# Another order of steps for the turn and the opening of the first attention

## The chip, the cores and the metric

The kernel runs on one core of one Trainium2 chip. The metric is the device time of one execution in microseconds (us), as the median over several runs. The engines are PE (TensorE), DVE (VectorE), ACT (ScalarE) and POOL (GpSimd); SP (SyncE) issues most of the DMAs. Each engine executes its own instruction stream in order and waits on semaphores.

## The reference

The program is a causal attention over 8 sequences of 512 tokens with 256 channels and 16 heads of 16, followed by a sum with the input and a layernorm, and then two layers of windowed attention and feed-forward. Only the first attention is touched:

```python
qkv = x @ w_qkv + b_qkv                      # x: 8 x 512 x 256
q, k, v = split_heads(jnp.split(qkv, 3))     # 16 heads of 16
a = (q @ k.T + causal_mask) / sqrt(16)
z = softmax(a) @ v
x = layernorm(x + (z @ w_out + b_out))
```

## The kernel before

The first attention handles one sequence (b = 0 to 7) at a time. Its work on a sequence is cut into named steps, and a step holds instructions for several engines. Steps that begin with `f_` belong to the "front" of the next sequence, the others to the sequence in hand. A loop of 7 turns executes the list `STEPS`; in it the front steps work for sequence b+1 while the rest finishes sequence b. Before the loop the list `OPENING` makes the front of sequence 0, and after it a list of joins finishes sequence 7 beside the first steps of the next stage. `follow` gives the same list to every engine: an engine takes the steps in the list's order and leaves out those in which it has nothing to do. So the list sets the order on each engine by hand, and nothing is reordered at run time.

The steps, with the engine's work in each:

- `f_x`: SP loads the sequence into `xin`; PE turns it (L576). `f_xe`: ACT writes `a_xt_hi` (L410), DVE `a_xt_lo` (L474).
- `f_qk:0` to `f_qk:3`: PE projects a quarter of q and k (L554 to L556), six matmuls each. `f_qe:i`: ACT makes `a_qk_hi` and `a_part_f` from it (L422, L426), POOL subtracts `a_qk_lo` (L371), and SP stores the three parts to the scratch tensor `qk_parts` (L304, L306).
- `f_load:i`: SP loads a quarter of the stacked `a_Q` and `a_K` from `qk_parts` (L322, four DMAs). Loads 0 and 1 need the stores of `f_qe:0` and `f_qe:1`, loads 2 and 3 those of `f_qe:2` and `f_qe:3`; in the loop, load i also waits until PE has finished the last `st` that reads the old quarter (`st:5`, `st:11`, `st:17`, `st:23`).
- `sm:i` and `f_sm:i` (32 of them): PE makes the scores of two heads for 128 queries (L631, mask L637) in one of two banks, DVE takes the negated maxima (L491). PE's `sm:i` waits for the maxima of `sm:i-2`. `f_sm:0`, `f_sm:8`, `f_sm:16` and `f_sm:24` wait for loads 0, 1, 2 and 3.
- `mt:i` and `f_mt:i`: PE turns the maxima (L663), ACT copies them to `a_mrow` (L445), SP puts them into `a_Q` (L327).
- `st:i` and `f_st:i` (24 of them): PE makes the scores again, turned (L676, L681), ACT takes the exponential into `a_PT` (L454). `ms:i` and `f_ms:i`: POOL masks blocks on the diagonal (L379).
- `pv:i` (4): PE multiplies by the values (L704). `z0:i` to `z3:i`: DVE turns and divides the result (L510, L512, L516), POOL (for the last one DVE) splits it (L384, L386), DVE turns it back (L529), ACT rounds it (L435).
- `f_v:i`: PE projects the values, DVE adds the bias (L497).
- `xr`: POOL loads the residual input, and DVE adds the output bias to it (L502). `out:i`: PE projects the output (L720, L722), DVE adds the residual (L536) and takes statistics. `end`: ACT normalises, POOL stores the rows.
- `nw` (opening only): SP loads the next stage's weights and stores rows of zeros.

PE, DVE and ACT share four single banks of PSUM; two of them (`FB`) serve the projections, `mt`, `pv` and `out` in turn, so that for example `f_qk:2` waits until ACT has read `f_qk:0` out.

Of the kernel before, what the change touches and what calls it, by code (L numbers as in the profile page):

```python
# [114 lines left out]
def parse(text):  # L115
    return [(name, int(i)) for name, i in (s.rsplit(":", 1) for s in text.split())]
# [67 lines left out]
def first_attention(nc, ctx, K, at, banks, scr, w, xin, rows_out, zeros, ahead, x, w_qkv, b_qkv, w_out, b_out, dst):  # L184
# [37 lines left out]
    xr = put(188480, "xr", [P, TB, DM])  # L222
    y, out = put(192576, "y", [P, TB, DM]), rows_out
    st, mv = sb("st", [P, TB, 6]), sb("mv", [P, TB, 2])
# [37 lines left out]
    GM, GE = PG * TB, PG * 3  # L262

    STEPS = parse("""
        f_xe:0 f_x:0 sm:27 st:8 sm:28 xr:0 mt:2 st:9 f_qe:0 f_qk:0 f_qk:1 f_qe:1 st:10 sm:29 ms:2 f_qk:2 ms:3
        f_load:0 sm:30 f_load:1 st:11 sm:31 f_qe:2 pv:0 st:12 z0:0 mt:3 f_qe:3 z1:0 f_qk:3 st:13 pv:1 f_sm:0
        st:14 f_sm:1 f_sm:2 st:15 f_sm:3 st:16 f_sm:4 st:17 f_sm:5 f_sm:6 st:18 f_sm:7 st:19 ms:4 f_sm:8 st:20
        z2:0 f_sm:9 f_sm:10 st:21 f_sm:11 ms:5 z0:1 ms:6 f_sm:12 st:22 z1:1 f_mt:0 f_sm:13 z3:0 st:23 z2:1
        pv:2 z0:2 f_sm:14 ms:7 z1:2 f_st:0 f_ms:0 f_load:2 f_load:3 f_sm:15 z0:3 pv:3 z3:1 z2:2 f_st:1 f_v:0
        z1:3 f_st:2 z3:2 f_mt:1 f_sm:16 z2:3 f_sm:17 f_st:3 f_v:1 f_sm:18 f_v:2 z3:3 f_sm:19 out:0 out:1  # L270
        f_sm:20 f_st:4 out:2 out:3 f_st:5 f_ms:1 f_sm:21 f_sm:22 f_st:6 f_sm:23 f_st:7 end:0 f_sm:24 f_v:3
        f_sm:25 f_sm:26""")
    FIRST = [s for s in STEPS if s[0][0] == "f"]
    OPENING = parse("""
        f_x:0 f_qk:0 nw:0 f_xe:0 f_qk:1 f_qk:2 f_qe:0 f_qk:3 f_qe:1 f_load:0 f_sm:0 f_sm:1 f_sm:2 f_sm:3
        f_qe:2 f_sm:4 f_sm:5 f_sm:6 f_qe:3 f_sm:7 f_load:1 f_load:3 f_sm:8 f_sm:9 f_sm:10 f_mt:0 f_ms:0
        f_sm:11 f_sm:12 f_v:0 f_sm:13 f_sm:14 f_st:0 f_sm:15 f_load:2 f_st:1 f_sm:16 f_sm:17 f_st:2 f_sm:18
        f_sm:19 f_mt:1 f_sm:20 f_st:3 f_sm:21 f_v:1 f_st:4 f_v:2 f_st:5 f_sm:22 f_sm:23 f_v:3 f_ms:1 f_st:6
        f_sm:24 f_sm:25 f_st:7 f_sm:26""")

    def sync(sp):
        sp.dma_start(xin[:, :, :], x[0].rearrange("(t p) d -> p t d", p=P)).then_inc(x_in, 16)
# [1463 lines left out]
def program(nc, t, out):  # L1746
# [7 lines left out]
    with ExitStack() as ctx:  # L1754
# [8 lines left out]
             for i in range(DEPTH)]  # L1763
# [4 lines left out]
                                   t["L0_ffn_ln_b"][i], t["L0_ffn_w1"][i], t["L0_ffn_b1"][i], t["L0_ffn_w2"][i],  # L1768
                                   t["L0_ffn_b2"][i]) for i in range(DEPTH)]
        stage, left = first_attention(nc, ctx, K, at, banks, scr, w[0], xin, rows_out, zeros, local[0], t["L0_attn_x"],  # L1770
                                      t["L0_attn_w_qkv"], t["L0_attn_b_qkv"], t["L0_attn_w_out"], t["L0_attn_b_out"],
                                      after_first)
# [44 lines left out]
```

## Time and profile before

| | us |
|---|---|
| median of 3 runs | 1787.78 (1783.2 to 1791.49) |
| the profiled execution | 1787.27 |
| its span in the profile | 1785.7 |
| PE busy | 1704.7 (95%) |
| DVE busy | 1150.5 (64%) |
| ACT busy | 997.9 (56%) |
| POOL busy | 866.6 (49%) |
| mean granted TensorE clock | 0.963 of full |

The opening takes the first 56 us, the seven turns of the loop run until about 446 us, and the rest belongs to the joins and the four stages behind. A turn is counted here from the first matmul of `f_x` to the next such matmul. "Full" clock is 2.4 GHz, and a granted clock of 0.50 is 1.2 GHz.

### The profile page before, as it was taken

What the parts mean: (1) busy time and instruction counts of PE and PEld (TensorE: products, weight loads), DVE (VectorE), ACT (ScalarE), POOL (GpSimd) and SP (SyncE); (2) the same over time, 40 slices, a digit from 0 to 9 for tenths busy, and PEclk for the clock granted to TensorE, in tenths of its full rate; (3) what the DMA queues carried; (4) which work ended last, traced back from release to release, by engine and by line L of the source; (5) the groups of instructions that cost most, each with busy time, mean ns of one, the idle gap of its engine ahead of it and who ended that gap; (6) DMA issues with size and microseconds to landing.
All of it is one profiled execution on the core that took longest, in us unless ns stands there. A gap on an engine that the chain in (4) does not pass through costs nothing.

```text
span 1785.7 us, 42024 instructions
## 1 busy us (share of the span) xinstructions
PE 1704.7 (95%) x13984; PEld 1305.2 (73%) x13984; DVE 1150.5 (64%) x2853; ACT 997.9 (56%) x1927; POOL 866.6 (49%) x886
## 2 busy tenths in 40 slices
PE   5999999999799999999989999899999999999997
PEld 3667566666477777777768888677777777778886
DVE  6678777787876676766643443876766776545554
ACT  2556576566545565555554555565555655655443
POOL 3343344434644665644643333556445656445453
PEclk7898898989989999999999999999999999999999
DMA  7454554544211011110023122101110010222221
GB/s 224 132 134 121 147 165 142 144 124 122 61 48 37 0 35 35 35 35 23 2 83 118 62 67 72 60 14 35 35 35 6 29 35 23 84 70 84 94 82 48
DMA packets 102327, 129.64 MB, mean 73 GB/s; under 512 B 15834, under 2 KB 70788, under 8 KB 102276
## 3 DMA queue, kind: packets, MB, share of 16 engines
q1 hardware_dynamic: 96084, 106.44, 20.5%
q0 software_dynamic: 6192, 22.55, 3.6%
q8 instruction: 29, 0.48, 0.1%
q14 instruction: 22, 0.18, 0.0%
HBM read 82.55 MB, written 46.15 MB: 72 GB/s over the span
## 4 chain that ended last, share of the span: by engine, by line
PE 81%; DVE 6%; DMA 4%; issue 3%; ACT 3%; POOL 1%; SPq 1%; DVEq 0%; POOLq 0%; ACTq 0%
PE b L1210 8%; PE d L1104 6%; PE b L1235 6%; PE d L1105 5%; PE d L1106 5%; PE d L631 3%; PE d L1151 3%; PE b L676 3%; PE d L1176 3%; PE b L704 3%; PE d L1623 2%; PE d L1625 2%; PE d L1624 2%; PE b L1250 2%; DMA a_K<-qk_parts 2%
## 5 line engine op out<-in xcount | busy, mean ns | idle before, releaser
L454 ACT ACTIVATE a_PT<-b 128x384 f32<-128x384 f32 (+1 forms) x384 | 183.6, 523 | 151.3 <-PE b L676 99.5
L491 DVE TENSOR_REDUCE a_negm<-d 128x2 f32<-128x256 f32 (+3 forms) x256 | 201.1, 814 | 67.1 <-PE d L637 65.3
L907 POOL TENSOR_TENSOR l_t<-l_t,l_t 128x512 f32<-128x512 f32 x128 | 165.0, 1297 | 113.4 <-DVE l_t L1059 113.3
L1077 DVE CUSTOM_DVE_ANT_0 d<-d,window 128x256 f32<-128x256 f32 (+1 forms) x512 | 184.4, 422 | 24.9 <-PE d L1176 24.6
L1476 POOL TENSOR_TENSOR m_hid_lo<-m_hid,m_hid_hi 128x512 fp32r<-128x512 f32 x80 | 103.3, 1301 | 161.6 <-ACT m_hid_hi L1537 161.5
L991 ACT ACTIVATE l_PT<-b 128x512 f32<-128x512 f32 (+1 forms) x256 | 125.3, 542 | 97.0 <-PE b L1218 95.0
L921 POOL TENSOR_TENSOR l_PS<-l_PT 128x768 f32<-128x768 f32 x64 | 117.6, 1838 | 111.4 <-ACT l_PT L991 111.4
L1104 PE MATMUL d<-w,l_xt 128*128 128x512 f32 x384 | 165.6, 431 | 4.8 <-DVE l_t L1059 4.7
L379 POOL TENSOR_SCALAR_AFFINE_SELECT a_PT<-a_PT 128x512 f32<-128x512 f32 x128 | 80.4, 656 | 180.3 <-ACT a_PT L454 179.6
L1105 PE MATMUL d<-w,l_xt 128*128 128x512 f32 x384 | 152.6, 398 | 0.0
L1106 PE MATMUL d<-w,l_xt 128*128 128x512 f32 x384 | 152.3, 397 | 0.0
L631 PE MATMUL d<-a_K,a_Q 63*128 63x256 f32 (+2 forms) x512 | 123.8, 449 | 24.3 <-DMA a_K<-qk_parts 18.0
L1210 PE MATMUL b<-l_Q,l_K 64*128 64x256 f32 x1536 | 139.2, 293 | 3.3 <-ACT l_PT L991 2.6
L1210 PEld LDWEIGHTS b<-l_Q,l_K 64*128 64x128 f32 x1536 | 108.8, 186 | 42.3 <-ACT l_PT L991 19.6
L914 POOL TENSOR_TENSOR l_qk<-l_t,l_inv 128x512 f32<-128x512 f32 x128 | 131.5, 1050 | 0.0
L1577 DVE SCALAR_TENSOR_TENSOR m_hid<-b,mw_b,m_gate 128x512 f32<-128x512 f32 (+1 forms) x48 | 35.9, 748 | 122.2 <-ACT m_gate L1524 97.3
L954 ACT ACTIVATE l_sq<-d 128x512 f32<-128x512 f32 x128 | 76.7, 599 | 65.5 <-PE d L1106 50.7
L1235 PE MATMUL b<-l_PT,l_V 128*64 128x256 f32 (+1 forms) x1024 | 112.2, 361 | 1.1 <-issue 0.7
L1054 DVE TENSOR_REDUCE l_ss<-l_sq 128x8 f32<-128x512 f32 x128 | 87.2, 681 | 31.2 <-ACT l_sq L954 30.6
L1094 DVE TENSOR_TENSOR rows_out<-b,l_xr 128x256 f32<-128x256 f32 x64 | 27.2, 425 | 123.6 <-PE b L1106 123.6
L1537 ACT ACTIVATE m_hid_hi<-m_hid 128x512 fp32r<-128x512 f32 x96 | 60.6, 631 | 75.1 <-DVE m_hid L1577 75.1
L925 POOL TENSOR_TENSOR l_zl<-l_zt,l_zh 128x512 fp32r<-128x512 f32 x64 | 81.5, 1294 | 39.7 <-ACT l_zh L997 39.7
(222 smaller groups left out, 4885.5 us busy)
## 6 DMA issues: line engine op xcount, KB each, us to landing
qk_parts<-a_qk_hi SPq DMA_DIRECT2D x64, 256.0 KB, 3.4
a_Q<-qk_parts SPq DMA_DIRECT2D x64, 192.0 KB, 3.7
a_K<-qk_parts SPq DMA_DIRECT2D x64, 192.0 KB, 4.6
qk_parts<-a_qk_lo SPq DMA_DIRECT2D x32, 256.0 KB, 4.0
xin<-after_attn SPq DMA_DIRECT2D x32, 256.0 KB, 3.1
m_xr<-after_attn SPq DMA_DIRECT2D x16, 512.0 KB, 3.9
after_attn<-rows_out POOLq DMA_DIRECT2D x14, 512.0 KB, 5.4
xin<-in_L_attn_x SPq DMA_DIRECT2D x8, 512.0 KB, 3.3
```

The source lines that it names most:

```text
L454: nc.scalar.activation(PT[:, p // PG % 2, 2 * (p % PG) + hh, QOFF[t]:QOFF[t] + nq], SC[hh][:, 0:nq], ACT.Exp, scale=AD ** -0.5).then_inc(e ...
L491: dve.tensor_reduce(negm[:, q, 2 * p:2 * p + 2], MX[i % 2][:, :, 0:nk], AX.X, ALU.max, negate=True).then_inc(max_done, 1)
L631: pe.matmul(bank[:, hh, 0:nk], Q[rows, p, P * q:P * q + P], Kk[rows, p, 0:nk], start=True, stop=True)
L907: pool.tensor_tensor(t1[:, par, w, :], t1[:, par, w, :], t2[:, par, w, :], ALU.add)\
L914: pool.tensor_tensor(qk[:, i, w, :].rearrange("p (h d) -> p h d", d=FD), t1[:, par, w, :].rearrange("p (h d) -> p h d", d=FD), inv[:, par, ...
L991: nc.scalar.activation(PT[:, p % 2, hh, j:j + 2, :].rearrange("p j q -> p (j q)")[:, 0:nq], SC[hh][:, 0:nq], ACT.Exp, scale=8.0).then_inc( ...
L1077: m = dve.tensor_tensor_reduce(out=o, in0=o, in1=mask, scale=-1.0, scalar=-NEG, op0=ALU.add, op1=ALU.min, accum_out=negm[:, q + t, p // 2, ...
L1104: pe.matmul(o, a_hi, r_hi, start=first, stop=False)
L1105: pe.matmul(o, a_lo, r_hi, start=False, stop=False)
L1106: return pe.matmul(o, a_hi, r_lo, start=False, stop=last)
L1210: pe.matmul(SC[hh][:, 2 * P * t:2 * P * t + 2 * P], lhs, rhs, start=(t == 0 and n == 0), stop=False, skip_group_check=True)
L1235: pe.matmul(OB[rows, P * j:P * j + nq], V[:, j, FD * h:FD * h + FD], PT[:, i % 2, hh, j, 0:nq], start=(j == 0), stop=(j == TB - 1), skip_g ...
```

## The change

Only the two lists differ. Every step of the old lists is in the new ones, and no instruction is added or removed.

```diff
     STEPS = parse("""
-        f_xe:0 f_x:0 sm:27 st:8 sm:28 xr:0 mt:2 st:9 f_qe:0 f_qk:0 f_qk:1 f_qe:1 st:10 sm:29 ms:2 f_qk:2 ms:3
-        f_load:0 sm:30 f_load:1 st:11 sm:31 f_qe:2 pv:0 st:12 z0:0 mt:3 f_qe:3 z1:0 f_qk:3 st:13 pv:1 f_sm:0
-        st:14 f_sm:1 f_sm:2 st:15 f_sm:3 st:16 f_sm:4 st:17 f_sm:5 f_sm:6 st:18 f_sm:7 st:19 ms:4 f_sm:8 st:20
-        z2:0 f_sm:9 f_sm:10 st:21 f_sm:11 ms:5 z0:1 ms:6 f_sm:12 st:22 z1:1 f_mt:0 f_sm:13 z3:0 st:23 z2:1
-        pv:2 z0:2 f_sm:14 ms:7 z1:2 f_st:0 f_ms:0 f_load:2 f_load:3 f_sm:15 z0:3 pv:3 z3:1 z2:2 f_st:1 f_v:0
-        z1:3 f_st:2 z3:2 f_mt:1 f_sm:16 z2:3 f_sm:17 f_st:3 f_v:1 f_sm:18 f_v:2 z3:3 f_sm:19 out:0 out:1
-        f_sm:20 f_st:4 out:2 out:3 f_st:5 f_ms:1 f_sm:21 f_sm:22 f_st:6 f_sm:23 f_st:7 end:0 f_sm:24 f_v:3
-        f_sm:25 f_sm:26""")
+        f_x:0 f_xe:0 sm:27 xr:0 st:8 mt:2 f_qk:0 f_qk:1 f_qe:0 f_qe:1 f_load:0 f_qk:2 ms:2 st:9 sm:28 f_load:1
+        sm:29 sm:30 st:10 ms:3 sm:31 f_qe:2 pv:0 st:11 mt:3 z0:0 st:12 z1:0 f_qk:3 st:13 f_qe:3 z2:0 pv:1 z0:1
+        st:14 f_sm:0 f_sm:1 st:15 f_load:2 f_sm:2 f_sm:3 st:16 f_sm:4 z1:1 z3:0 st:17 ms:4 f_sm:5 f_sm:6 st:18
+        ms:5 f_sm:7 st:19 f_sm:8 st:20 f_sm:9 ms:6 f_sm:10 f_mt:0 st:21 f_sm:11 f_sm:12 ms:7 st:22 f_load:3
+        f_sm:13 z2:1 f_sm:14 z0:2 st:23 pv:2 z1:2 f_sm:15 f_sm:16 z0:3 pv:3 z3:1 f_st:0 z2:2 f_v:0 f_mt:1 z1:3
+        f_st:1 z3:2 f_sm:17 z2:3 f_v:1 f_st:2 f_sm:18 z3:3 f_v:2 f_st:3 f_sm:19 out:0 f_st:4 f_sm:20 out:1
+        out:2 out:3 f_st:5 f_sm:21 f_ms:0 f_ms:1 f_sm:22 f_st:6 f_sm:23 f_st:7 f_sm:24 f_v:3 end:0 f_sm:25
+        f_sm:26""")
     FIRST = [s for s in STEPS if s[0][0] == "f"]
     OPENING = parse("""
-        f_x:0 f_qk:0 nw:0 f_xe:0 f_qk:1 f_qk:2 f_qe:0 f_qk:3 f_qe:1 f_load:0 f_sm:0 f_sm:1 f_sm:2 f_sm:3
-        f_qe:2 f_sm:4 f_sm:5 f_sm:6 f_qe:3 f_sm:7 f_load:1 f_load:3 f_sm:8 f_sm:9 f_sm:10 f_mt:0 f_ms:0
-        f_sm:11 f_sm:12 f_v:0 f_sm:13 f_sm:14 f_st:0 f_sm:15 f_load:2 f_st:1 f_sm:16 f_sm:17 f_st:2 f_sm:18
-        f_sm:19 f_mt:1 f_sm:20 f_st:3 f_sm:21 f_v:1 f_st:4 f_v:2 f_st:5 f_sm:22 f_sm:23 f_v:3 f_ms:1 f_st:6
-        f_sm:24 f_sm:25 f_st:7 f_sm:26""")
+        f_x:0 f_xe:0 f_qk:0 f_qe:0 f_qk:1 f_qk:2 f_qk:3 f_sm:0 f_sm:1 f_sm:2 f_qe:1 f_load:0 f_sm:3 f_sm:4
+        f_sm:5 f_qe:2 f_load:1 f_qe:3 f_sm:6 f_sm:7 f_ms:0 nw:0 f_sm:8 f_mt:0 f_sm:9 f_sm:10 f_sm:11 f_sm:12
+        f_sm:13 f_st:0 f_sm:14 f_st:1 f_sm:15 f_sm:16 f_load:2 f_st:2 f_sm:17 f_st:3 f_sm:18 f_v:0 f_st:4
+        f_sm:19 f_ms:1 f_load:3 f_mt:1 f_sm:20 f_sm:21 f_sm:22 f_v:1 f_st:5 f_v:2 f_sm:23 f_sm:24 f_st:6 f_v:3
+        f_st:7 f_sm:25 f_sm:26""")
```

## Rows read from the trace of the kernel before

**Rows 1.** The page's granted clock in 40 slices of the span, tenths of full speed

```profile
PEclk7898898989989999999999999999999999999999
```

**Rows 2.** Windows: turns 1, 2 and 4, and the sum of turns 1 to 6

```profile
core 0: us, PE busy (x) PEld busy (x) DVE busy (x) ACT busy (x) POOL busy (x), PEclk, DMA share, GB/s
56.05:114.92 58.87, 55.13 (x491) 36.84 (x489) 40.73 (x69) 34.44 (x70) 19.93 (x30) 0.86 0.47 127
114.92:170.44 55.52, 53.95 (x488) 36.31 (x489) 40.92 (x70) 34.70 (x71) 22.50 (x32) 0.88 0.51 142
...
226.93:279.33 52.40, 50.43 (x488) 33.25 (x489) 40.59 (x70) 34.45 (x71) 22.46 (x32) 1.00 0.52 151
...
sum 335.96, PE 322.58 PEld 213.12 DVE 245.13 ACT 207.78 POOL 132.27; mean PE 53.76 PEld 35.52 DVE 40.85 ACT 34.63 POOL 22.05
```

**Rows 3.** Waits of PE in the loop: us in total, times, longest

```profile
PE d L631 <- DMA a_K<-qk_parts: 9.3, 7, 3.4
PE d L631 <- DVE a_negm L491: 3.4, 15, 0.3
PE b L676 <- DMA a_Q<-a_mrow: 0.5, 1, 0.5
```

**Rows 4.** Timeline of PE: head of turn 2, `f_sm:0` of turn 4 (start, us, instruction, idle)

```profile
114.92 1.09 PE L576 MATMUL b<-ident,xin 128*128 128x128 f32 x8
...
118.21 0.50 PE L554 MATMUL b<-a_xt_hi,w 128*128 128x512 f32 x1
...
121.16 0.45 PE L676 MATMUL b<-a_Q,a_K 64*128 64x384 f32 x2
...
123.33 0.44 PE L631 MATMUL d<-a_K,a_Q 63*128 63x384 f32 x2
...
124.45 0.51 PE L631 MATMUL d<-a_K,a_Q 63*128 63x512 f32 x2 [0.29 <-DVE a_negm L491]
...
130.12 2.36 PE L704 MATMUL b<-a_PT,a_V 128*32 128x512 f32 x32
133.48 0.38 PE L631 MATMUL d<-a_K,a_Q 63*128 63x256 f32 x2 [1.00 <-DMA a_K<-qk_parts]
...
245.24 0.38 PE L631 MATMUL d<-a_K,a_Q 63*128 63x256 f32 x2 [0.76 <-DMA a_K<-qk_parts]
```

**Rows 5.** Timeline of DVE in turn 2, head

```profile
116.24 1.29 DVE L474 TENSOR_TENSOR a_xt_lo<-b,a_xt_hi 128x512 fp32r<-128x512 f32 x2 [0.16 <-ACT a_xt_hi L410]
...
122.35 1.45 DVE L502 TENSOR_TENSOR a_xr<-a_xr,a_bo 128x1024 f32<-128x1024 f32 x1 [3.36 <-DMA a_xr<-in_L_attn_x]
```

**Rows 6.** Timeline of ACT in turn 2: the second copy of `f_qe:0`

```profile
120.58 0.68 ACT L426 ACTIVATE a_part_f<-b,a_bqk 128x512 f32<-128x512 f32 x1
```

**Rows 7.** Timeline of POOL in turn 2: `end`'s store, subtractions of `f_qe:0` and `f_qe:1`

```profile
116.38 0.86 POOL L398 DMA_DIRECT2D after_first<-rows_out  x1 [1.82 <-ACT rows_out L440]
...
121.42 3.50 POOL L371 TENSOR_TENSOR a_qk_lo<-a_part_f,a_qk_hi 128x512 fp32r<-128x512 f32 x2 [3.17 <-ACT a_part_f L426]
```

**Rows 8.** Timeline of SP in turn 2: last store of `f_qe:1`, first of `f_load:0`

```profile
125.09 0.33 SPq L306 DMA_DIRECT2D qk_parts<-a_qk_lo  x1
127.33 0.89 SPq L322 DMA_DIRECT2D a_Q<-qk_parts  x2
```

**Rows 9.** Windows from `f_sm:0` to `pv:2` on PE, turns 2 and 4

```profile
133.48:148.32 14.84, 14.83 (x116) 11.33 (x116) 12.15 (x18) 9.95 (x20) 3.67 (x7) 0.57 0.46 138
...
245.24:257.32 12.08, 11.63 (x116) 8.07 (x117) 10.83 (x16) 9.39 (x20) 3.17 (x6) 1.00 0.53 166
```

**Rows 10.** Timeline of DVE in turn 4, `f_sm:0` to `pv:2`

```profile
245.74 3.62 DVE L491 TENSOR_REDUCE a_negm<-d 128x2 f32<-128x256 f32 x5 [4.88 <-PE d L637]
249.99 3.02 DVE L491 TENSOR_REDUCE a_negm<-d 128x2 f32<-128x512 f32 x4 [0.63 <-PE d L637]
252.92 0.70 DVE L529 STREAM_TRANSPOSE a_ztf<-a_on 128x512 f32<-128x512 f32 x1
...
256.21 0.71 DVE L510 STREAM_TRANSPOSE a_ot<-b 128x512 f32<-128x512 f32 x1
256.95 0.26 DVE L512 RECIPROCAL a_rc<-a_ot 128x16 f32<-128x16 f32 x1
```

**Rows 11.** Timeline of PE in the opening: `f_sm:16`

```profile
43.50 0.58 PE L631 MATMUL d<-a_K,a_Q 63*128 63x256 f32 x2 [0.86 <-DMA a_K<-qk_parts]
```

## The prediction

> **What bounds the kernel now.** I read the page first: PE is busy for 95% of the span, so only what PE waits for, and the clock at which it works, can give time back. The line of the granted clock [rows 1] shows where that is: the slices below 9 lie in the first 400 us, the opening and the loop of the first attention, which are all that the change touches. I therefore cut the loop into its turns [rows 2]. Turn 4 takes 52.40 us at a clock of 1.00; turns 1 and 2 take 58.87 and 55.52 us at 0.86 and 0.88. All have the same work, and PE calls itself busy in the extra time too. The first six turns sum to 335.96 us, and six times 52.40 is 314.4: 21.6 us are lost against the turn without a low clock. By the same view five of the seven turns have a stretch at 0.50, always between `f_sm:0` and the first matmuls of `pv:2`, and turns 4 and 7 have none.
>
> Then I asked what PE waits for in the loop [rows 3]. One wait stands out: 9.3 us in seven waits for the DMA into `a_K`, that is `f_sm:0` waiting for `f_load:0`. One of them, in turn 1, is 3.4 us, the other six average (9.3-3.4)/6 = 0.98. The next is DVE, 3.4 us in 15 small pieces. In turn 2 [rows 4] the wait is 1.00 us ahead of 133.48, right where the dense projections and `pv:1` end and the thin 63-row matmuls begin.
>
> **Step 1: the new head of a turn.** All times here are us from the turn's first matmul, in turn 2 (114.92) [rows 4]. Before, `f_qk:0` starts at 3.29 and `f_sm:0` at 18.56, with waits of 0.29 (`sm:31`) and 1.00 in between. In the new list `sm:28` and `st:9` move behind `f_qk:2`, `st:11` behind `pv:0`, and `st:14` ahead of `f_sm:0`. That is the same work plus `st:14`. Three new waits appear:
>
> - `f_qk:0` needs `a_xt_lo`, whose second half ends at 116.24+1.29, or 2.61 [rows 5]. PE is there at about 2.4 now. A wait of 0.2 to 0.3, and `f_qk:0` starts at about 2.75, 0.55 earlier.
> - `f_qk:2` follows `f_qk:1` directly and needs the second copy of `f_qe:0`, which ended at 121.26 [rows 6], 3.05 behind the start of `f_qk:0`. The two projections between take 121.16-118.21 = 2.95 [rows 4], and a signal needs some 0.1. A wait of 0.1 to 0.2, which `st:10` and `sm:29` covered before.
> - DVE has `xr:0` ahead of `sm:28` now. Its addition waits for a DMA until 7.43 and ends at 8.88 [rows 5]. The maxima of `sm:28` (about 0.4) end at 9.3, and PE needs them for `sm:30`, which it reaches at about 8.5. A wait of 0.8 to 0.9. Queued behind the addition are all later maxima; `sm:31` comes right after with nothing more to wait for.
>
> Together 1.1 to 1.4. I take 1.3; the lower bound is 0.4, if the residual lands at once, and the upper one 2.6, if it lands 1.24 later (rival 3). The step `xr` on POOL comes behind `f_ms:0` and `f_ms:1` now, where one of them stood before; that is 1.24 us more on POOL, hidden in the 1.82 us in which it waited for ACT's normalised rows [rows 7].
>
> **Step 2: the load.** `f_load:0` is ready when the stores of `f_qe:1` have landed. Its chain is `f_qk:0`, ACT, the two subtractions on POOL (3.50 us, stretched while the addition of `xr` runs beside them) [rows 7], the store at 125.09, and 2.24 us until SP issues the load at 127.33 [rows 8], then 6.15 until `f_sm:0` runs. I let the chain move with `f_qk:0`: 0.55 earlier, so the data is there at 18.56-0.55 = 18.0. PE gets there at 18.56-1.00-0.29+1.3+0.45 (`st:14`, by the `st` at 121.16 [rows 4]) = 19.0. The wait is gone, with 1.0 us to spare. SP stays in order: `f_load:1` waits for `st:11` and holds the stores of `f_qe:2` behind it, but SP is occupied by the first load's four issues until then, as before. `f_load:2` and `f_load:3` are issued 9 and 2 steps of scores earlier and are needed at `f_sm:16` and `f_sm:24`; they gain cover.
>
> The head alone is thus no gain: 1.3 of new waits against 0.98+0.29 = 1.27 of old ones. Only turn 1 gains, where of 3.4 about 1.4 stays and some 0.4 of new waits is added (its `xr` is early): -1.6.
>
> **Step 3: between `f_sm:0` and `pv:2`.** In turn 4 this stretch takes 12.08 us and DVE is busy for 10.83 of them [rows 9]; its maxima run in chains of 3.02 us per four, with `z2:0` (0.70) and `z0:1` (0.71 and 0.26) among them [rows 10]. These 1.67 us move ahead of `f_sm:0`, where DVE lay idle for 4.88 us [rows 10]. Against it stand `f_sm:14`, now inside the stretch, and that `z0:1` has to wait for `pv:1` and so delays the first maxima of `f_sm:0` by up to 0.3. For equal work I get 0.3 to 0.5 less than before. The tail behind `pv:3` has the same matmuls against the same DVE work. Its swaps (`f_st`, `f_mt:1`, `out:1`) are covered as long as the additions into `a_V`, `z3:3` and the maxima are done before PE asks; without that cover they cost up to 0.5 a turn. Head, middle and tail together lie between -0.3 and +0.7 a turn; I take the middle, +0.2, or +1.4 for seven turns.
>
> **Step 4: the clock.** This is the main term. The low stretch makes `f_sm:0` to `pv:2` 14.84 us in turn 2 against 12.08 in turn 4 [rows 9]. Of the 21.6 us lost, 2.6 are turn 1's longer wait; the rest, 19.0 in five turns, is 3.8 a turn. In the trace each fall comes in the thin stretch behind the stall, in no turn before it, and a turn with nearly the same stall (0.76 in turn 4 [rows 4]) keeps full speed. So the trace bears out that these turns are close to the edge, and not that the stall alone decides. Two things now make the stretch denser: no DMA wait at its start, and 1.67 us less of DVE's work inside. I expect four of the five falls to go, -15.2, with none (0) and all (-19.0) as bounds. The Trainium skill says in "TensorE: Matmul & The Clock Gate", section "HAM oscillation — how this bites in real kernels", that waits for DMAs between short runs of matmuls are what puts the array back to half rate; by that rule all five would go, and the sum would be 3.8 lower.
>
> **Step 5: the opening.** `f_sm:16` loses its 0.86 us wait for `f_load:2` [rows 11], since more scores stand between `f_mt:0` and it. Moving `nw` back takes its two large loads away from the first stores, but by the time these are issued the loads had landed; nothing. `f_load:1` overtakes the stores of `f_qe:3`, needed only much later. -0.9, within -2 and +1.
>
> **The sum.** The profiled execution took 1787.3 (span 1785.7), half a microsecond from the median of 1787.8. +1.4 (turns 1 to 7), -1.6 (turn 1), -15.2 (clock), -0.9 (opening) is -16.3: 1771. The joins are as they were and begin with the same steps finished.
>
> **The rivals.**
>
> *Rival 1: the low clock stays.* The new waits of step 1 are smaller but three, and the thin stretch itself is the same matmuls. For it: turns 4 and 2 differ by only 0.24 us of stall. Against it: the turn that fell latest (turn 3) fell behind further small waits, one of them of 0.5 for `a_mrow` [rows 3], which now has more cover. Time: 1787.3+1.4-1.6-0.9 = 1786. The skill's page has a section "A second HAM failure mode: psum-queue depth-cycling", by which frequent short idle times between groups of matmuls are enough to make the clock oscillate; it speaks for this rival, and the full-speed turn 4 with its small waits for DVE speaks against its always being so.
>
> *Rival 2: half of it.* Two or three of the five falls go: -9.5 instead of -15.2, 1777.
>
> *Rival 3: slower.* DVE's queue behind the residual. If the residual lands later than 7.43, each microsecond is one more for PE at `sm:30`, in six turns. If POOL's 1.24 us are not hidden, that is +7.4; and if the idle time now in the head lets the clock fall in all seven turns, two more at 3.8 are +7.6. 1786+15 = 1801. It decides once the head loses over 1.7 us a turn beyond step 1 and the clock gives nothing, or half of that with seven falls. For it: the addition already waited 3.36 us [rows 5]. Against it: POOL's wait of 1.82.
>
> **How the numbers follow.** About 0.5%, or 9 us, is what a measurement of this kernel tells from no change. Forecast 0.42, rival 1 0.22, rival 2 0.25, rival 3 0.11. The forecast and four fifths of rival 2 lie more than 9 us below: faster 0.61. Rival 1 and the rest of rival 2 are the same, 0.28; slower 0.11. The range reaches from 1763 (all falls gone, -19.0, and turns 0.3 shorter, -2.1, with the rest as above) to 1790, which holds rivals 1 and 2 with some microseconds for the phase of the clock in other stages. The likeliest case's own range is 1766 to 1777.
>
> **What would show it.** The DMA wait at `f_sm:0` near zero in turns 2 to 7 (step 2); new idle time of PE at `f_qk:2` and at `sm:30`, the latter with DVE's L502 just before (step 1); turns of 52 to 53 us with a clock of 1.00 in at least five of seven, against two before (step 4); `f_sm:0` to `pv:2` below 12.1 us in them (step 3). The prediction is wrong if turns at full clock take over 53.5 us, which would mean that I missed a wait, or if half the turns or more still show 0.50.

## The result: no gain, and a little slower

The changed kernel took 1792.76 us in the median of 12 runs (1779.94 to 1803.25), the kernel before 1786.12 in 12 runs beside it (1778.85 to 1791.93). The ratio is 1.004, with a 95% interval of 1.002 to 1.0059, or some 7 us more (3.6 to 10.5). I had forecast 1771 within 1763 to 1790. The profiled execution of the changed kernel took 1801.12 (span 1799.6) and is itself 8 us above the median; the profile of before lies 1 us above its own.

The page's granted clock in 40 slices, to be held against [rows 1]:

```profile
PEclk7788989988999999999999999999999999999999
```

The windows of turns 1 to 6 of the changed kernel, in the columns of [rows 2]:

```profile
60.92:118.30 57.38, 55.11 (x492) 35.57 (x489) 40.50 (x70) 34.05 (x70) 18.93 (x29) 0.88 0.44 121
118.30:176.48 58.18, 55.77 (x488) 35.07 (x489) 41.06 (x70) 34.65 (x71) 21.41 (x33) 0.88 0.48 136
176.48:230.89 54.41, 51.97 (x488) 33.04 (x489) 41.12 (x70) 34.64 (x71) 21.41 (x33) 0.97 0.52 145
230.89:289.60 58.71, 56.28 (x489) 35.87 (x489) 41.50 (x70) 34.66 (x71) 21.42 (x33) 0.85 0.46 135
289.60:343.95 54.35, 51.93 (x488) 32.85 (x489) 41.24 (x70) 34.64 (x71) 21.40 (x33) 0.97 0.51 145
343.95:401.92 57.97, 55.59 (x489) 35.04 (x489) 41.03 (x70) 34.68 (x71) 21.43 (x33) 0.88 0.46 136
sum 341.00, PE 326.65 PEld 207.44 DVE 246.44 ACT 207.31 POOL 125.99; mean PE 54.44 PEld 34.57 DVE 41.07 ACT 34.55 POOL 21.00
```

The six turns sum to 341.00, against 335.96. No turn has a clock of 1.00 any more; even the two best, 3 and 5, have 0.97 and take 54.4, against 52.40 in turn 4 of before. What PE waits for in the loop, as in [rows 3]:

```profile
PE d L631 <- DVE a_negm L491: 9.7, 8, 1.6
PE b L663 <- DVE a_xt_lo L474: 0.9, 6, 0.2
PE b L676 <- DMA a_Q<-a_mrow: 0.9, 1, 0.9
PE d L631 <- DMA a_K<-qk_parts: 0.3, 1, 0.3
```

The 9.3 us for the DMA into `a_K` are gone, as meant. In their place stand 9.7 us for DVE's maxima, where 3.4 stood. The timeline of turn 3 shows where (this turn begins at 176.48). PE first, from `f_qk:2` on, to be read beside [rows 4]:

```profile
182.23 0.50 PE L554 MATMUL b<-a_xt_hi,w 128*128 128x512 f32 x1
...
186.35 0.44 PE L631 MATMUL d<-a_K,a_Q 63*128 63x384 f32 x2 [1.55 <-DVE a_negm L491]
...
187.45 4.05 PE L704 MATMUL b<-a_PT,a_V 128*32 128x512 f32 x32
```

Then DVE and POOL in the same head, beside [rows 5, 7]:

```profile
183.85 2.11 DVE L502 TENSOR_TENSOR a_xr<-a_xr,a_bo 128x1024 f32<-128x1024 f32 x1 [3.63 <-DMA a_xr<-in_L_attn_x]
185.88 3.11 DVE L491 TENSOR_REDUCE a_negm<-d 128x2 f32<-128x256 f32 x4
```

```profile
182.35 2.53 POOL L371 TENSOR_TENSOR a_qk_lo<-a_part_f,a_qk_hi 128x512 fp32r<-128x512 f32 x2 [2.63 <-ACT a_part_f L426]
```

Two things are to be seen. At `sm:30` PE stands still for 1.55 us until DVE has finished the addition and the maxima of `sm:28`. And `pv:0` right behind it takes 4.05 us, where the same 32 matmuls took 2.36 [rows 4]: the granted clock is 0.50 there. Both are so in turns 2 to 7 (in turn 5 `pv:0` takes 3.87). In turn 1 the residual is there early, the wait is 0.25, and `pv:0` keeps full speed. Besides, the middle of the turn, from `f_sm:0` to `pv:2`, still has its low stretch in five of the seven turns, as before; they are now turns 1, 2, 4, 6 and 7, and were 1, 2, 3, 5 and 6.

The clock's part can be read from every run, not only from the profiled one. It has two levels, 1.00 and 0.50, so a run's low time is twice (1 - mean granted clock) times its span. The mean low time is 121.0 us in 113 runs of the kernel before (standard error 1.2) and 125.2 in 12 of the changed one (4.6).

### The profile page after: what moved, and what is told of

It is laid out like the page before. It is cut to its first block, busy times and chain, and to the rows that moved or that the text cites. A ratio compares the mean times of both kernels' runs of the same rounds, so it can differ in the third digit from the quotient of the medians.

```text
span 1799.6 us, 42024 instructions
## 1 busy us (share of the span) xinstructions
PE 1715.9 (95%) x13984; PEld 1301.8 (72%) x13984; DVE 1153.1 (64%) x2853; ACT 997.9 (55%) x1927; POOL 860.2 (48%) x886
## 4 chain that ended last, share of the span: by engine, by line
PE 80%; DVE 6%; DMA 4%; issue 4%; ACT 3%; POOL 2%; SPq 1%; POOLq 0%; DVEq 0%; ACTq 0%
PE b L1210 8%; PE b L1235 6%; PE d L1104 6%; PE d L1105 5%; PE d L1106 5%; PE b L704 4%; PE d L1151 3%; PE b L676 3%; PE d L631 3%; PE d L1176 2%; PE d L1623 2%; PE d L1625 2%; PE d L1624 2%; PE b L1250 2%; DMA a_xr<-in_L_attn_x 2%
## 5 line engine op out<-in xcount | busy, mean ns | idle before, releaser
L631 PE MATMUL d<-a_K,a_Q 63*128 63x256 f32 (+2 forms) x512 | 115.2, 442 | 22.9 <-DVE a_negm L491 12.8
L1104 PEld LDWEIGHTS d<-w,l_xt 128*128 128x128 f32 x384 | 72.6, 189 | 38.9 <-issue 18.1
```

The lines of the kernel that those rows point to most:

```text
L631: pe.matmul(bank[:, hh, 0:nk], Q[rows, p, P * q:P * q + P], Kk[rows, p, 0:nk], start=True, stop=True)
L1104: pe.matmul(o, a_hi, r_hi, start=first, stop=False)
```

## The experiments

Each kernel's times stand beside runs of the kernel before on the same chip, whose medians lay between 1785 and 1788. A "low time" is a mean over the kernel's runs, with its standard error behind it.

**One part alone.** The first kernel has the old turn and the new opening, the second the new turn and the old opening.

> The old turn with the new opening. Theory 1 (the new opening itself costs: in the profile after, the loop began at 60.92 us and not at 56.05, with the low clock lasting until 62 us and not 51): 4 to 5 us slower than before, about 1791, and the profile again shows the loop beginning near 61. Rival (the later rise of the clock was chance in that one execution): within 2 us of before, and a loop that begins at 55 to 57.

Measured: 1787.24, ratio 1.0017 (0.9996 to 1.0039); low time 126.6 (5.4). PE waits 8.0 us for `a_K`, against 9.3 before, and no head has a low stretch at `pv:0`. The time is that of the rival, but the loop begins at 60.81, as theory 1 said; I come back to this at step 5.

> The new turn with the old opening. Theory 1 (the turn costs about 2 us in sum over seven turns, the opening the rest of 6.6): about 1788, 2 us over before, with the wait of 1.5 us of PE at sm:30 and a stretch at half clock behind it in six turns. Rival (the turn is the whole loss): about 1793.

Measured: 1792.14, ratio 1.0037 (1.0017 to 1.0057); low time 120.0 (4.0). The profile has the waits and the low heads of the changed kernel:

```profile
PE d L631 <- DVE a_negm L491: 10.0, 9, 1.6
```

So the turn alone makes the kernel slower, as the rival said. The opening is within its error of nothing here.

**The addition behind `sm:31`.** The changed kernel with DVE's half of `xr` as a step `xb` of its own, so that `sm:28` to `sm:31` no longer stand behind it on DVE. The same step stands in the joins behind the loop, where the order stays.

```diff
-        sm:29 sm:30 st:10 ms:3 sm:31 f_qe:2 pv:0 st:11 ...
+        sm:29 sm:30 st:10 ms:3 sm:31 xb:0 f_qe:2 pv:0 st:11 ...
```

> The changed kernel, but DVE's addition into a_xr (L502) is a step of its own and comes behind sm:31; POOL still issues its load at the old place. Theory A (the addition ahead of sm:28 makes PE wait 1.5 us at sm:30, and the idle time then lets the clock fall, so that pv:0 takes 4.05 us in place of 2.36): both go, 1.55 + 1.69 = 3.2 us in six turns, 19 us less than the changed kernel, about 1774, and pv:0 takes 2.36 in all turns. Theory B (the clock falls in the head because the thin steps sm:28 to sm:31 now stand together, whatever the wait): only the 1.55 goes, about 1784, and pv:0 stays at about 4.

Measured: 1783.18, ratio 0.9995 (0.9972 to 1.0019), about 8 us below the changed kernel by the ratios; low time 119.4 (6.1). PE's waits for DVE's maxima fall to 2.5 us, none over 0.4. No head is low, and `pv:0` takes 2.36, as theory A said. But 8 us is less than half of its 19. The heads of the profile lose about 20 us of low time (3.4 in each of six), and the mean run only 6, so low time seems to come back elsewhere, within large errors. The addition now runs clear of POOL's subtractions:

```profile
179.95 1.54 DVE L502 TENSOR_TENSOR a_xr<-a_xr,a_bo 128x1024 f32<-128x1024 f32 x1
```

A turn without a low stretch takes 51.5, in the windows of turns 4 and 6 of this kernel:

```profile
223.68:275.16 51.48, 50.32 (x488) 32.64 (x489) 40.84 (x70) 34.65 (x71) 21.56 (x33) 1.00 0.55 153
...
329.46:381.15 51.69, 50.21 (x488) 32.62 (x489) 40.94 (x70) 34.64 (x71) 21.54 (x33) 1.00 0.55 153
```

The head's wait and its low stretch went together, and what came back is about the whole loss of 7 us. But with neither DMA wait nor DVE wait left, the low time is still that of the kernel before. The middle keeps its low stretches, three of seven in this profile.

**The same with the old opening.**

> The turn of e3_addition_late (addition behind sm:31) with the old opening. If what the opening costs (about 3 us) and what the addition costs (about 8 us) add up: 1780, 0.3% faster than before. If the opening's cost was chance: as e3, 1783.

Measured: 1781.3, ratio 0.9985 (0.9961 to 1.0008); low time 119.1 (4.9), and low stretches in the middle of six turns of its profile. The time lies between the two that I had expected and decides for neither.

**A projection between `sm:29` and `sm:30`.** The changed kernel with `f_qk:2` put there.

> The changed kernel with f_qk:2 between sm:29 and sm:30, and the addition where the change put it. Theory A: the projection's 1.4 us fill PE's wait, and the clock stays up in the head; about 1775 to 1778, pv:0 at 2.36. Theory B: the wait is filled as well, and thin steps are now parted by a dense one, so B also says a full clock. Against both: if f_qe:2, now 2 us later, holds back f_load:2, a DMA wait shows at f_sm:16, and the gain is smaller.

Measured: 1798.66, ratio 1.0062 (1.0038 to 1.0085). My expectation was wrong in its reasoning: the work that PE does before `sm:30` is the same in either order, so the wait stayed (10.3 us in all, 1.7 at most). `f_qk:2` only came later. The middle is low in all seven turns of this profile.

**The kernel before, with the addition ahead of `sm:28`.**

```diff
-        ... sm:27 st:8 sm:28 xr:0 mt:2 ...
+        ... sm:27 xr:0 st:8 sm:28 mt:2 ...
```

> The kernel before with one step moved: xr ahead of sm:28, so that DVE's addition stands ahead of the maxima of sm:28 as in the changed kernel. Theory A (that order alone makes PE wait and the clock fall in the head): PE waits for DVE about 1 us at sm:29 or sm:30 in six turns and pv:0 takes over 2.4 us in some; 6 to 15 us slower than before. Rival (the wait only matters because the changed turn puts the projections together ahead of it; here the DMA wait at f_sm:0 shrinks by what PE loses earlier): within 3 us of before.

Measured: 1787.64, ratio 1.0004 (0.9983 to 1.0026); the waits for DVE rise from 3.4 to 6.1, none over 0.8, and no head is low. This is what the rival said: the order on DVE alone, without the projections at the head of the turn, costs nothing that is measured.

**`pv:0` ahead of `sm:30`.** The changed kernel with a block of PE's work that needs nothing of DVE's put in front of the wait.

> The changed kernel with pv:0 ahead of sm:30 in place of behind sm:31; the addition stays ahead. In e4 the projection was moved from one place ahead of sm:30 to another, which gives PE no more to do before it, so its wait stayed at 1.7 us. Here 2.3 us of other work come ahead of sm:30. Theory A: the wait of 1.5 us and the low clock in the head both go, as with e3: about 1784. Theory B (thin steps together): sm:28 to sm:31 are parted as well, so B also says a full clock; if the clock still falls at the same place, both are wrong.

Measured: the 12 runs fall into two groups, six from 1770.5 to 1788.4 and six from 1805.3 to 1808.2 at a clock of 0.951 or 0.952. The ratio of 0.9975 (0.9943 to 1.0008) is over the first six alone; the median over all is 1796.82. Why there are two groups I don't know. In the profile, which is of the first group, the waits for the maxima fall to 0.6 us, another of 0.66 a turn for ACT comes up at `mt:3`, and a turn at full clock takes 52.2. `pv:0` keeps full speed and no middle is low, but in three of seven turns the clock falls behind the new wait of 0.66. The spread makes it no use as a repair.

**Half of the addition.** The changed kernel with the bias added to 512 of the 1024 columns only (the other half goes without).

> The changed kernel with DVE's addition of the output bias to the residual done on half of the columns only (512 of 1024; the other half is left without the bias). The addition takes 2.11 us beside POOL's subtractions and comes down to about 1.1. Theory A (PE's wait at sm:30 is the addition's length on DVE, and the fall of the clock in the head comes with that wait): the wait falls by 1.0 a turn, from 1.6 to about 0.5 (10 us in the loop to about 3.5), the low stretch in the head goes, pv:0 takes 2.36 instead of 4.05, and the kernel is 8 to 10 us faster than the changed one, about 1783. Rival B (it is the late landing of the residual that PE waits for, or the clock falls for another reason): the wait falls by less than 0.5 a turn, the head keeps its low stretch in most turns, and the time stays within 3 us of the changed kernel's.

Measured: 1779.1, ratio 0.9962 (0.9934 to 0.9989); low time 101.8 (6.4). The heads' low stretches are gone and a turn at full clock takes 52.21, as theory A said. But the wait at `sm:30` fell by 0.53, from 1.55 to 1.02, and not by 1.0. DVE and then POOL in turn 3 of this kernel show why:

```profile
178.47 1.67 DVE L502 TENSOR_TENSOR a_xr<-a_xr,a_bo 128x512 f32<-128x512 f32 x1 [3.56 <-DMA a_xr<-in_L_attn_x]
180.06 3.11 DVE L491 TENSOR_REDUCE a_negm<-d 128x2 f32<-128x256 f32 x4
```

```profile
177.05 2.54 POOL L371 TENSOR_TENSOR a_qk_lo<-a_part_f,a_qk_hi 128x512 fp32r<-128x512 f32 x2 [2.65 <-ACT a_part_f L426]
```

The half addition, 0.68 in turn 1 where POOL is elsewhere, takes 1.67 here. It ends 180.14-179.59 = 0.55 behind the end of POOL's second subtraction. The whole one in the changed kernel ends 185.96-184.88 = 1.08 behind it. So the addition is not just slowed down; it stands still until POOL is through, and then needs nearly its own time (1.22 for the whole one in turn 1). All turns say the same. In turns 2 to 7 of the changed kernel it starts between 7.27 and 7.51 behind the turn's first matmul and always ends 1.08 behind POOL's second subtraction. In the kernel before it starts between 6.98 and 7.43 and always ends 1.08 behind the first one. Even the late addition, 1.54 above, ends 181.49-180.42 = 1.07 behind a mask block of POOL's.

**Dense work in the middle.** The turn of the late addition with the old opening, and `f_qk:3` with `f_qe:3` moved behind `st:16`; `f_load:2` and `f_sm:16` go later for it.

> As e6, and the dense projection f_qk:3 (with f_qe:3) moves into the thin stretch, behind st:16; f_load:2 and f_sm:16 move later so that their loads are there in time. Theory C (the clock falls between f_sm:0 and pv:2 because that stretch is long and thin, whatever stands before it): no or one low stretch there in seven turns, 10 to 19 us less than e6, about 1765. Theory D (the falls are the after-effect of waits ahead of the stretch): as many falls as in e6 and no gain, about 1780, or slower if f_sm:16 now waits for its load.

Measured: 1788.28, ratio 1.0025 (1.0004 to 1.0046); low time 109.1 (3.1), 10 less than without the move. But five of seven turns of the profile still have a low stretch in the middle, as theory D said, PE waits 9.0 us for ACT's exponentials now, and the turns are longer. In two turns the clock also falls over `pv:1`, behind a wait of 0.43 for ACT. Not decisive.

**The scores twice, in the kernel before.** In the loop PE makes the scores of `f_sm:0` to `f_sm:13` twice, the second time over the first. All waits and all other work stay.

```diff
-                    pe.matmul(bank[:, hh, 0:nk], Q[rows, p, P * q:P * q + P], Kk[rows, p, 0:nk],
-                              start=True, stop=True)
+                    for again in range(2 if name == "f_sm" and i < 14 and not isinstance(b, int) else 1):
+                        pe.matmul(bank[:, hh, 0:nk], Q[rows, p, P * q:P * q + P], Kk[rows, p, 0:nk],
+                                  start=True, stop=True)
```

> The kernel before, but in the loop PE makes the scores of f_sm:0 to f_sm:13 twice (the second time over the first), so the middle stretch holds 28 more 63-row matmuls a turn, which nothing needs. They take 0.1 to 0.2 us each at full clock: about +4 us a turn, +28 in all, if PE sets that stretch, and less where it waited for DVE anyway. Theory A (the clock falls in the middle because PE has too little to do there, and the DMA wait at its start has no part in it): the DMA wait of about 9 us stays, yet two or fewer of the seven turns keep a low stretch in the middle, against five; the low time of the whole run falls from 119 us towards 85, and the time comes out near 1786+28-12 = 1802. Rival B (the DMA wait or something outside the stretch brings the falls): five to seven turns keep them, low time 119 or more, 1814.

Measured: 1776.45 in 5 runs (1770.51 to 1779.27), ratio 0.9939 (0.9917 to 0.9962). More work, none of it needed, makes the kernel 11 us faster by the ratio, where both theories had it slower. Low time: 63.1 (3.7), against 121.0. The wait for the DMA in the loop, to be held against [rows 3]:

```profile
PE d L632 <- DMA a_K<-qk_parts: 9.2, 7, 4.2
```

The page's granted clock, against [rows 1]:

```profile
PEclk7899999999899999999999999999999999999999
```

The windows of turn 2 and of its stretch from `f_sm:0` to `pv:2`, against [rows 2, 9]:

```profile
115.16:168.16 53.00, 51.33 (x516) 34.50 (x517) 40.21 (x70) 34.38 (x71) 22.43 (x32) 1.00 0.53 149
...
133.47:146.20 12.73, 12.63 (x148) 9.42 (x152) 11.03 (x17) 9.39 (x20) 3.26 (x6) 1.00 0.48 156
```

The DMA wait is untouched, and the low stretch is gone from all turns but the first. The second scores cost 12.73-12.08 = 0.65 in the stretch, not the 4 that I expected. So PE had room there for 28 more matmuls, although the profile calls it busy for 11.63 of the 12.08 us without them [rows 9]: not all of its busy time is work. This is the run that settles the main term: with waits of about 1 us for the load and more work on PE behind them, the middle keeps its clock. Turn 1 is the exception. Its wait for the load is 4.17 us long, and the clock falls within it.

**The scores twice in the changed kernel,** with the new opening and then with the old one.

> The changed kernel with f_sm:0 to f_sm:13 of the loop made twice by PE, as was done to the kernel before. Theory A (the falls in the middle come from PE having little to do between f_sm:0 and pv:2; the fall in the head comes with the wait for DVE's addition and is another one): the middle falls go in at least five of seven turns, the wait of 1.6 at sm:30 and the 3.4 us low stretch in the heads stay. The middle stretch gets about 1 us a turn longer at full clock (+7) and loses some 2.8 us in each turn that fell (five: -14): about 1785 against 1793. Rival B (the changed turn is long in the middle for a reason of its own order): the falls stay, 1793 to 1800.

Measured: 1780.56 in 10 runs, ratio 0.997 (0.9948 to 0.9991); low time 71.5 (2.6). No low stretch is left in the middle of any turn, and the waits for DVE stay (11.1 us, 1.6 at most). But only two of the six heads behind such a wait are low now. In turn 3 the same wait stands ahead of a `pv:0` at full speed:

```profile
176.07 0.44 PE L632 MATMUL d<-a_K,a_Q 63*128 63x384 f32 x2 [1.55 <-DVE a_negm L491]
...
177.17 2.36 PE L705 MATMUL b<-a_PT,a_V 128*32 128x512 f32 x32
```

So the fall in the head went with the wait in the run with the late addition, but the wait by itself doesn't bring it. What else does isn't shown. The window of turns 2 and 3 together, both at full clock:

```profile
112.52:219.92 107.40, 102.38 (x1032) 67.94 (x1033) 82.33 (x139) 69.25 (x141) 42.72 (x65) 1.00 0.54 147
```

That is 53.7 a turn, against 53.15 in the mean of turns 2 to 6 for the order of before under the same edit.

> The changed turn with f_sm:0 to f_sm:13 made twice and the old opening. The kernel before with the same edit took 1776, and with both of the change's parts 1781. Theory A (the opening costs some 4 us and the changed turn, with the falls in the middle out of the way, is worth the DMA waits that it removes less the wait at sm:30, which about cancel): 1776 to 1778. Rival B (the opening costs nothing and the turn costs all): 1781.

Measured: 1781.31 in 7 runs, ratio 0.9954 (0.9935 to 0.9974); low time 69.6 (3.0). With the same opening and the same edit, the turn of before took 1776.45. The changed turn costs 4.9 us by the medians and 2.7 by the ratios, whose intervals overlap. In the two profiles turns 1 to 6 sum to 324.29 and 324.67, so they don't show it. The opening, 1780.56 against 1781.31, costs nothing by the medians and 2.9 us by the ratios. Rival B is the nearer one.

**The scores between, and then twice as well.** The turn of the late addition with the old opening, and `st:9` between `f_qk:1` and `f_qk:2`, to cover PE's wait for ACT there. In turn 3 of the kernel with the late addition PE's weight load stands still for 0.50 there, and the matmuls behind it come about 0.2 late.

```diff
-        ... f_load:0 f_qk:2 ms:2 st:9 sm:28 ...
+        ... f_load:0 ms:2 st:9 f_qk:2 sm:28 ...
```

> The changed turn with the addition behind sm:31 and the old opening, and now also st:9 between f_qk:1 and f_qk:2, to cover the wait of 0.50 for ACT's second copy that stands there. Theory A (each wait of PE in the head counts in full): 0.4 us a turn less than the same kernel without it, -3 us: 1778, ratio to the kernel before about 0.996. Rival B (PE reaches the next wait earlier and the time is given back, at f_sm:0 or to DVE): 1781, ratio 0.998 to 0.999, and the idle time turns up at another row.

Measured: 1777.84 in 12 runs (1760.6 to 1790.5), ratio 0.9952 (0.9928 to 0.9975) and low time 100.1 (7.1) without the two longest, 106.6 (7.3) with them. The spread goes with the clock: single runs lie between 0.961 and 0.985. So it says little on the 0.4 us a turn that I meant to test. The profile is of the fastest run, 1760.6, and only one of its middles is low; turns 2 to 6 take 51.5.

> The turn with the addition behind sm:31 and st:9 between f_qk:1 and f_qk:2, with the old opening, and f_sm:0 to f_sm:13 of the loop made twice. Theory A (falls in the middle follow PE's load there): low time falls to about 60 to 70 us in every run, clock 0.98 or more each time, and the time is 1763 to 1770, below the 1778 of the same kernel without the second scores. Rival B (with the wait in the head gone the falls are rare enough that the added work costs as much as it saves): 1775 to 1780.

Measured: 1766.63 in 4 runs (1766.54 to 1766.97), ratio 0.9873 (0.9841 to 0.9906); low time 57.4 (1.7). This beats both kernels, by 1.3% and more, and by 9.8 us the kernel before with its scores made twice. The second scores aren't free: turns 2 to 6 take 52.5 at full clock, 1.0 more than without them, and the fastest run without them is 6 us faster than these four. They pay because without them the clock seldom stays up.

> The turn with the late addition, st:9 between the projections and f_sm:0 to f_sm:13 made twice, but with the new opening in place of the old one. The clock hardly falls in this turn and the same kernel with the old opening lay at 1766.5 to 1767.0, so this prices the opening. Theory A (the new opening costs time by itself, since PE reaches the loop later, 60.9 against 56.0 us in the profiles of the changed kernel and the kernel before): 1770 to 1772. Rival B (where PE enters the loop says nothing, because the opening leaves less behind, and the opening costs nothing): 1766 to 1768.

Measured: 1766.35 in 4 runs (1763.66 to 1770.37), ratio 0.988 (0.9853 to 0.9906). The opening costs nothing here by the medians, and 1.3 us by the ratios.

## Why the prediction was wrong

**What bounds the kernel.** PE and its clock: right. The reading of the DMA wait as what tips the clock was the error, though the two stood side by side in five turns of seven.

**Step 1, the head.** The waits before `f_qk:0` and `f_qk:2` came as sized: 0.15, taken at `mt:2`, and some 0.2. The one at `sm:30` was at the right place with the right instruction in front of it, but 1.55 and not 0.8 to 0.9. The three come to 1.9 and not 1.3, within the bound of 2.6. The residual was not late: the addition starts 7.37 behind the turn's first matmul, and I had 7.43. It takes 2.11, and not 1.45. In [rows 5, 7] DVE's addition (122.35) arrives during POOL's first subtraction, waits for its end and runs ahead of the second, and then POOL is held up: two subtractions in 3.50 instead of 2.53. I wrote that POOL was "stretched while the addition of `xr` runs beside them" and did not ask what happens when the order turns. The projections come 0.6 earlier, the subtractions with them, from 6.50 to 5.87 behind the turn's start. Now the residual lands during POOL's second one, and DVE has to wait for the end of that: the addition ends 9.48 behind the turn's start instead of 8.88. The Trainium skill states this in "SBUF — State Buffer", section "SBUF: two separate sides": GpSimd and a DVE operation with two inputs in SBUF take one pair of ports as an exclusive lock, whoever comes first keeps it for the whole instruction, and the other stands. The trace agrees, by the 1.08 and 0.55 above. I did not weigh it.

The second half of the error is what I did not price in the forecast: the clock in the head. The stall and what stands around it bring the low level over `pv:0`, 4.05 instead of 2.36, or 1.7 a turn. With a wait of 1.02 (half the addition), or 0.4 at most (late addition), the heads stay at full speed. With 1.55 and the scores made twice, two and three heads of six are low.

The rest of the head, middle and tail was forecast at +0.2 a turn. A turn with its head low and the rest at full clock takes 54.4; less 1.7 that is 52.7, against 52.40, or +0.3. Take 1.2 of the wait away too, and it is 51.5, which the kernel with the late addition shows. So the sum of the steps on work and waits was right, but by two errors that cancel: the head's new waits are 0.6 more than forecast, and the rest of the turn some 0.5 less. In turn 3 two waits are gone that PE had in the middle of turn 4 before, 0.28 for the maxima and 0.21 ahead of `pv:3`.

**Step 2, the load.** Right: 9.3 us became 0.3. Turn 1 came out 1.5 shorter, where I had 1.6, but that is chance: 0.3 of its wait stayed and not 1.4, and a wait of 0.91 for `a_mrow` came up behind it.

**Step 3, the middle.** Not seen apart, since the stretch holds other steps now; by the sum just given, middle and tail together came out some 0.5 a turn shorter than forecast.

**Step 4, the clock.** This step failed, and with it the forecast. I expected four of five falls in the middle to go, -15.2; as many remained in the profile, and the low time of the whole run went from 121.0 to 125.2 instead of falling. Its evidence was a coincidence in time: each fall came behind the stall. The counterexample was in the rows, turn 4 with a stall of 0.76 at full clock [rows 4], and I explained it as being "close to the edge". The trace had a plainer pair, turns 6 and 7:

```profile
354.73 0.38 PE L631 MATMUL d<-a_K,a_Q 63*128 63x256 f32 x2 [0.75 <-DMA a_K<-qk_parts]
...
410.48 0.38 PE L631 MATMUL d<-a_K,a_Q 63*128 63x256 f32 x2 [0.91 <-DMA a_K<-qk_parts]
```

Turn 6 has the shorter stall and fell (its clock is 0.88 in the mean), and turn 7 kept full speed. The rule of the Trainium skill in "TensorE: Matmul & The Clock Gate", section "HAM oscillation — how this bites in real kernels", by which waits for DMAs put the array back to half rate, would have had all five go. The waits in the case that the Trainium skill describes there are several times as long as 1 us. No run here bears the rule out for waits of 1 us; in turn 1 of the kernel before with the scores twice the clock does fall inside a wait, of 4.17. Without the waits of 1 us the falls stayed (low time 119.4 and 119.1), and with them, but with more work for PE, they went (63.1). The size of the term was about right: the kernel before with the scores twice gained 11 us by the ratio and paid 53.15-52.40 = 0.75 a turn, 5.3 in seven, for the added work, so the clock was worth some 16, for 58 us less of low time. The clock was to be had by another change than the one I priced.

**Step 5, the opening.** Forecast at -0.9. By the ratios the new opening costs 0.5 us in the changed kernel, 3.0 where it stands alone, 1.8 with the late addition, and 2.9 and 1.3 in the two pairs with the scores twice. Each is within its error, but all point the same way. PE enters the loop later in the profile, 60.92 against 56.05, where the low stretch of the opening lasts until 61.5 instead of 50.2; where it ended earlier (48.8, in the last kernel) PE entered at 56.6. So that is the clock again. Over all the profiles, eight with the new opening enter the loop at 59.5 in the mean (56.6 to 61.0) and nine with the old one at 57.2 (55.7 to 59.7), and the low stretch lasts beyond 56 in six of the eight and in one of the nine. So my estimate is that the new opening costs about 2 us, and that most of it goes with a longer low stretch, where I had a gain of 0.9. Why the stretch lasts longer isn't shown.

**The account.** Six turns are 5.0 longer: +0.3 in each (1.8), the low heads of turns 2 to 6 (8.5), turn 1 without its wait beyond that (-1.8, taken from its measured length), and four low stretches in the middle instead of five (-3.8, by the price of step 4) make 4.7. The rest of the 13.9 between the two profiled spans lies in the opening (4.9) and behind turn 6 (4.0), and half of it is the draw, since the medians are 6.6 apart.

**The rivals.** Rival 1, the low clock stays, named what happened in the middle; its 1786 lacks the low heads and the longer wait before them. Rival 3 named the place and DVE's queue behind the addition. It had the residual late, where it was the port, and it wanted 3.8 for each fall in the head, where one costs 1.7. I gave it 0.11, though its queue on DVE stood in my own step 1.

**What stays open.** Why a middle falls in one turn and not in the next, the work being the same. That more work for PE takes the falls away is shown: in the five profiles with the scores twice one middle in 35 turns is low, and in the other twelve 51 in 84. But those twelve go from none (`pv:0` ahead of `sm:30`) to all seven, and a projection moved into the middle left five of seven, so neither what decides between turns nor which work counts is shown. Nor is the low head, with the same wait ahead of it in all of six turns or in two. Nor did I try to separate the length of the stall in the head from the work around it, beyond the lengths above.

## What to carry to other kernels

Where the clock falls behind a wait, don't put a price on the wait before a turn with the wait and without the fall is explained: add work for PE that nothing needs, and see whether the fall goes. When a transfer or an engine is brought forward, look at each pair of operations on DVE and POOL that now changes its order, since an addition here stood still until POOL's subtraction was done, and POOL until the addition was. A stall of PE in front of a run of dense matmuls is priced with the low clock that may stand behind it, here up to 1.7 us with a stall of 1.55 and none with one of 1.02.

## What the runs showed of the hardware that I had not expected

Adding 28 matmuls a turn to a PE that calls itself busy for 95% of the time made the kernel 0.6% faster. With the mended order it is 1.3% faster, of which the order alone gives 0.5%. Four runs of that kernel lie within 0.4 us, where the kernel before spreads over 13; with the new opening four spread over 6.7, so how much of the spread goes isn't settled. In the changed kernel the low level comes over `pv:0` with a stall of 1.55 in every one of six turns, with 1.02 in none; with the scores twice the same 1.55 brings it in two or three of six. And a DVE addition that meets a running POOL subtraction ends 1.08 us behind that subtraction (0.55 for half of the columns), whenever it started.
